# Second attention: a chunk's softmax weights behind the next chunk's rotated rows, their transposes behind its scores

## The reference, cut to what matters

```python
Q = (x @ Wq).reshape(B, T, h, k).transpose(0, 2, 1, 3)
K = (x @ Wk).reshape(B, T, g, k).transpose(0, 2, 1, 3)
V = (x @ Wv).reshape(B, T, g, k).transpose(0, 2, 1, 3)
...
Q = Q * cos + rotate_half(Q) * sin
K = K * cos + rotate_half(K) * sin
scores = jnp.einsum('bhqk,bhsk->bhqs', Q, K) / jnp.sqrt(jnp.float32(k))
scores = jnp.where(causal[None, None], scores, -jnp.inf)
A = jax.nn.softmax(scores, axis=-1)
Y = jnp.einsum('bhqs,bhsk->bhqk', A, V)
...
h = h + _L1_attn_ref(_layernorm(h, axis=-1), ...)
```

## Time and profile before

| | |
|---|---|
| runs before, us | 1389.83 median of 3 (1388.47 to 1391.47) |
| the profiled execution, us | 1393.95, its span 1391.8 |
| TensorE matmuls busy | 1228.5 us, 88% of the span |
| VectorE, ScalarE, GpSimd busy | 864.6, 613.2, 231.8 us |
| TensorE busy from 1040 to 1190 us (the second attention) | 115.45 of 150 us, mean granted clock 0.78 |
| VectorE busy there | 104.86 of 150 us |

### The profile page before, as it was taken

The page is one execution under the profiler, slowest core; times in us unless marked ns, Lnnn a source line. Parts: engine busy times, 40 slices in busy tenths (PEclk is TensorE's granted clock), DMA queues, the critical chain, the costliest instruction groups (busy, mean ns, idle before and its releaser), DMA issues.

```text
span 1391.8 us, 30551 instructions
## 1 busy us (share of the span) xinstructions
PE 1228.5 (88%) x10764; PEld 718.6 (52%) x10778; DVE 864.6 (62%) x1767; ACT 613.2 (44%) x1054; POOL 231.8 (17%) x280
## 2 busy tenths in 40 slices
PE   5999899999999999957799999999957885959997
PEld 2447566666666666635344444444524664424443
DVE  5985454655546555488844454554357677778886
ACT  3444444544445444425244444444423332246664
POOL 2220000000000000000123333333258600110000
PEclk9997999999999999986999999999977887989998
DMA  5121452444524435214147767775247700000000
GB/s 196 61 83 49 154 202 109 181 175 162 198 109 181 181 145 210 107 46 185 46 150 251 265 218 279 262 253 183 92 129 135 105 7 2 1 1 16 23 23 27
DMA packets 43277, 180.98 MB, mean 130 GB/s; under 512 B 9172, under 2 KB 10512, under 8 KB 35408
## 3 DMA queue, kind: packets, MB, share of 16 engines
q0 software_dynamic: 19744, 95.41, 20.7%
q1 hardware_dynamic: 20016, 72.15, 14.6%
q10 hardware_dynamic: 3456, 12.58, 2.5%
HBM read 132.39 MB, written 47.73 MB: 129 GB/s over the span
## 4 chain that ended last, share of the span: by engine, by line
PE 52%; DVE 24%; issue 13%; ACT 4%; POOL 2%; DMA 2%; DVEq 1%; another core or an unknown queue 0%; SPq 0%; ACTq 0%; POOLq 0%
PE ps L935 14%; PE ps L937 13%; PE ps L936 13%; DVE rs L1611 2%; PE ps L1049 2%; DVE ff L2043 2%; DVE amf L2050 2%; PE ps L1028 1%; PE ps L1123 1%; PE ps L1376 1%; DVE we_sp L1405 1%; DVE bst L1478 1%; PE ps L1264 1%; ACT vp L682 1%; PE ps L1358 1%
## 5 line engine op out<-in xcount | busy, mean ns | idle before, releaser
L935 PE MATMUL ps<-nT_hi,wa_hi 128*128 128x368 f16 x576 | 189.2, 328 | 11.8 <-DVE wa_lo L1405 7.7
L936 PE MATMUL ps<-nT_lo,wa_hi 128*128 128x368 f16 x576 | 188.8, 328 | 0.0
L937 PE MATMUL ps<-nT_hi,wa_lo 128*128 128x368 f16 x576 | 188.1, 327 | 0.0
L1772 DVE SCALAR_TENSOR_TENSOR nrm<-ps,xg,nrm 128x256 f32<-128x256 f32 x61 | 29.5, 483 | 122.9 <-ACT nrm L749 103.1
L523 POOL DMA_INDIRECT xg<-xrow,idx x61 | 61.2, 1004 | 263.4 <-PE ps L1123 113.8
L935 PE MATMUL ps<-wide,xT 128*128 x244 | 92.7, 380 | 13.8 <-issue 9.3
L1605 DVE SCALAR_TENSOR_TENSOR a<-sq,eps_row,E 128x184 f32<-128x184 f32 x32 | 13.1, 409 | 131.3 <-ACT sq L699 131.3
L1579 DVE SCALAR_TENSOR_TENSOR wide<-ps,wide 128x368 f32<-128x368 f32 x128 | 66.8, 537 | 42.0 <-PE ps L937 42.0
L936 PE MATMUL ps<-wide,xT 128*128 x244 | 92.5, 379 | 0.0
L937 PE MATMUL ps<-wide,xT 128*128 x244 | 92.5, 379 | 0.0
L1358 PE MATMUL ps<-qw,qT 128*128 128x512 bf16 x372 | 85.6, 383 | 4.0 <-DVE ff L2043 2.6
(11 more groups left out here) (317 smaller groups left out, 2893.6 us busy)
## 6 DMA issues: line engine op xcount, KB each, us to landing
we_st<-in_we POOLq DMA_DIRECT2D x16, 1536.0 KB, 6.8
wsp<-we_sp POOLq DMA_DIRECT2D x16, 1536.0 KB, 5.4
wide<-wsp SPq DMA_DIRECT2D x16, 1536.0 KB
yslot<-yt POOLq DMA_DIRECT2D x61, 256.0 KB
wq_st<-in_ffq SPq DMA_DIRECT2D x24, 512.0 KB, 4.5
wq_st<-in_ffq ACTq DMA_DIRECT2D x24, 512.0 KB, 3.5
wide<-in_wa SPq DMA_DIRECT2D x10, 1024.0 KB, 6.9
xt<-in_x SPq DMA_DIRECT2D x12, 512.0 KB, 3.5
```

The lines of the kernel that those rows point to most:

```text
L935: nc.tensor.matmul(dst, lhs[0], rhs[0], start=start, stop=False)
L936: nc.tensor.matmul(dst, lhs[0], rhs[1], start=False, stop=False)
L937: return nc.tensor.matmul(dst, lhs[1], rhs[0], start=False, stop=stop)
L1772: V.scalar_tensor_tensor(ht, ps[:, 2 + p, FI:2 * FI], AS / WS if x is None else xgw[:, x, ds(D + e, 1)], sgt[:, p, :], ALU.mult, ALU.mult) ...
```

## The change

Only orders change; no instruction is added, removed or resized. In chunks 1 to 3 VectorE's `weights(c - 1)` moves from before rotation 2 to behind `rotated(c)` and the row tiles' `low`, just ahead of `centred(c)`. In chunks 1 and 2 `group_stats` moves ahead of rotation 1, `group_shift` stands behind rotation 1 (and `y_low`), and `low(k)` behind rotation 3. On TensorE `turn(c - 1)` moves behind `scores(c)`, the row turns k+1 and k+2 come directly behind the value projection and lose their wait for ScalarE's evictions of the weights, and the turn waits for `low` of tile k+2 in place of k. ScalarE empties the row turns before the weights' turns. Chunk 0 and the turn of the last chunk stay as they are.

```diff
@@ ScalarE
                 moved(c, 5)
-                if c:
-                    weights_turned(c - 1)
                 if inner:
                     high(k + 1)
                     high(k + 2)
...
+                if c:
+                    weights_turned(c - 1)
                 if c + 1 < CH:
                     moved(c + 1, 0)
                     moved(c + 1, 1)
@@ TensorE
-                if c:
-                    turn(c - 1, k if inner else NT - 1)
                 if inner:
-                    for j in (k + 1, k + 2):
-                        pe.wait_ge(f_pe, ready(4 * (c - 1) + 2 + j % 2))
-                        row_turn_l1(j)
+                    row_turn_l1(k + 1)
+                    row_turn_l1(k + 2)
...
                 scores(c)
+                if c:
+                    turn(c - 1, k + 2 if inner else NT - 1)
                 if c + 1 < CH:
@@ VectorE
                 rotate(c, 0)
+                if inner:
+                    group_stats(c + 1)
                 rotate(c, 1)
...
                 if c > 1:
                     y_low(c - 2)
-                if c:
-                    if c + 1 < CH:
-                        group_stats(c + 1)
-                        group_shift(c + 1)
-                    weights(c - 1)
-                for j in range(2, 5):
-                    rotate(c, j)
-                    if j == 2 and 0 < c < CH - 1:
-                        low(k)
+                if inner:
+                    group_shift(c + 1)
+                rotate(c, 2)
+                rotate(c, 3)
+                if inner:
+                    low(k)
+                rotate(c, 4)
                 rotated(c)
...
+                if c:
+                    weights(c - 1)
                 centred(c)
```

More of the change, by code:

```diff
@@ L1947, in _ @@
                 k = GT * (c + 1)
+                inner = 0 < c < CH - 1
                 rotate(c, 0)
+                if inner:
+                    group_stats(c + 1)
                 rotate(c, 1)
@@ L1955, in _ @@
                     y_low(c - 2)
-                if c:
-                    if c + 1 < CH:
-                        group_stats(c + 1)
-                        group_shift(c + 1)
-                    weights(c - 1)
-                for j in range(2, 5):
-                    rotate(c, j)
-                    if j == 2 and 0 < c < CH - 1:
-                        low(k)
+                if inner:
[5 more added lines that the diff above has]
+                rotate(c, 4)
                 rotated(c)
-                if 0 < c < CH - 1:
+                if c == 0:
+                    group_shift(1)
+                    low(k)
+                if inner or c == 0:
                     low(k + 1)
                     low(k + 2)
[L1969 to L1972, removed]
+                if c:
+                    weights(c - 1)
                 centred(c)
```

## The result

The changed kernel took 1382.32 us (median of 5, 1377.17 to 1383.52) and the kernel before 1391.47 us in the same set of runs; the ratio is 0.9942 with a 95% interval of 0.9925 to 0.9959, so 8.1 us faster (5.7 to 10.4). The medians alone lie 9.2 us apart; I go by the ratio. A second set gave 0.9945 (0.9925 to 0.9966). The forecast was 1383.8 us, a gain of 6.0 us.

A forecast was written before the change was run, and what follows sets the result against it. In the second attention TensorE and VectorE wait for each other in a loop, neither full, with the weights in its path. Chunks 1 to 3 gain 1.1 + 2.6 + 2.3 = 6.0 us: 1389.83 - 6.0 = 1383.8; 8-in-10 range 1380.8 to 1388.2.

The forecast's parts named there:

- VectorE, chunk 2: VectorE's new order in chunk 2 releases the scores 15.5 us after the first rotation (20.9 before); chunk gains 2.6 us in all.
- R: Start of VectorE's first rotation in chunk 2, at 1115.18 before, from which the forecast counts.
- Chunk 3: Rotated rows come earlier and the turn fits into the 3.56 us wait ahead of `weighted`: 2.3 us gained (3.2 to -1.0).
- Chunk 1: Wait before row turn k goes; 0.3 us lost by order, 1.1 gained with the clock's 1.4 (range 3.0 to -1.1).
- Statistics earlier: Chunks 1 and 2, VectorE: statistics start about 4 us behind the last addition's issue; listed among edits that cost nothing.
- at nothing: Forecast's list of moved steps given no gain or cost: later `low(k)`, earlier statistics and root, ScalarE's order.
- The turn and the clock: Turn behind the scores costs 3.83 us; its transposes bring back full clock for the next projection, 1.4 us each in chunks 1 and 2.
- Behind chunk 3: From chunk 3's `weighted` to the output rows: nothing changes, the gain arrives whole, 0 us added.
- (a): Rival: transposes do not raise TensorE's clock, projections stay slow; 3.2 us gained, 1386.6 us; chance 0.14.
- (b): Rival: gain does not show, eaten by the `rotated` wait, late weights or issue gaps; at most 2 us, some 1388.5; chance 0.12.
- (c): Rival: slower, TensorE's clock stays low from the scores on; up to 5.5 us lost, 1395.3; chance 0.08.
- It would wait for `h`, up to 2 us once: Chunk 2, VectorE: earlier statistics wait if the last addition into `h` lands later than about 4 us behind its issue.

The follow-up runs named there:

- threefold turn: Changed kernel with each transpose of the turns behind chunks 1 to 3's scores issued three times; stage 115.5 us, run once for its profile.
- TensorE's order alone: Kernel before with TensorE and ScalarE in the new order, VectorE in the old one; 9.9 us slower than before (6.4 to 13.5).
- early split: Changed kernel with last chunk's weights ahead of chunk 2's low parts, output weights' split ahead of chunk 2's first rotation; ratio 0.9901 to the kernel before.
- projection first in chunk 2: Kernel with last weights first and output weights' split early, plus chunk 2's next projection ahead of the turn; ratio 0.9890 to the kernel before, median 1376.62 us.

## Why the prediction was right, and where it was off

The direction and the size hold: 6.0 us forecast, 8.1 (5.7 to 10.4) measured, 8.5 in the stage. That the time itself came within 1.5 us of 1383.8 is in part luck: the kernel before ran at 1391.47 in this set and not at the 1389.83 that I took off from.

*VectorE, chunk 2.* Right to 0.1 us: `rotated` at R + 15.5, the weights at R + 20.6 (forecast 20.7), the next projection at 24.4 (forecast 24.5), the new wait for `qp` 1.86 (forecast 1.7).

*Chunk 3.* Right: 2.1 for 2.3. The scores ran slower than taken (5.44 for 4.7), `rotated` came a little sooner (13.2 us behind the first rotation for 13.5), the turn hid in the wait.

*Chunk 1* was the term mis-sized, 2.3 for 1.1. I left the value projection at its 6 us; it took 2.9. The scores took 3.77 where I had 6.2. Two waits on VectorE (1.01 and 1.34) took back part of both, as the sum for chunk 2 would have told me had I worked out chunk 1 in the same way. So did the clock behind chunk 0, where nothing was changed: it stayed at 1.2 GHz for 5.7 us of the projections (1074.2 to 1079.9) where it had for 2.5 before (1081.7 to 1084.2), and row turn k came 20.6 us behind the mask, where the sum has 19.2.

*Statistics earlier* stood among the edits "at nothing", with the root's 0.99 and the row turns' 1.2 to 1.4 counted elsewhere and partly traded for the wait for `qp`. Alone it gave 5.8 us (3.6 to 8.2). With the weights late it decides between 110.3 and 104.9 us of stage. This is the larger error: by the sum the gain is chiefly the weights', and the runs give the statistics at least as much of it. By themselves the statistics took 4.7 us off the stage and the weights with the turns 3.1 (timed 5.8 and 4.6, with intervals that overlap); on top of the other they took 5.4 and 3.8.

*The turn and the clock.* The turn cost 3.8 us as taken, and transposes do bring the clock back, as the threefold turn shows; but in chunks 1 and 2 it came back only behind the turn, 2.5 and 1.4 us into the first projection (1101.34 to 1103.80, 1129.67 to 1131.07), so projection and eviction took 4.0 and 3.5 us where 4.6 had been: 0.6 and 1.1 gained for the 1.4 taken twice. What was missing there came in at the scores, at 3.77 and 4.01.

*Behind chunk 3* I forecast nothing and 1.5 us came: `weighted` 1.65 for 2.33, the last turn 3.43 for 3.83, and the last `weighted` 1.7 for some 2.2, all by a higher clock (1.00, 0.58 and 1.00 granted, where it was 0.50, 0.50 and 0.55).

*The signs.* Two of those that I had named went the other way. The turn waited 1.34 and 1.10 us for the weights, where over 1 us was to speak against the forecast: the scores ran faster than taken and no longer covered the weights. And the granted clock was 0.62 and 0.72 over the first projections behind the turns of chunks 1 and 2, not 1.00 in most of both.

*The rivals.* (a) fell by the threefold turn as a mechanism, though of the time that the clock was to give back (1.4 twice) only 1.7 us came. (b), nothing shows, fell; its reason, that VectorE's list leaves little slack, is true, as the waits for `qp` and the weights show. (c) did not come about, though TensorE's order alone shows that it exists. "It would wait for `h`, up to 2 us once" was not met in the changed kernel, and met with 3.3 us as soon as the rotation came 4.4 us earlier. I had counted the margin of 4 us from the issue and not from the landing: with the rotation 0.7 and 1.4 us earlier (early split, projection first in chunk 2) the third tile's statistics already waited 0.26 and 1.09 us.

## What to carry to other kernels

When two engines wait for each other in turn, write each one's list as a sum from one fixed event to the next (here R + 15.5, R + 20.7) for every chunk; that sum was right to a tenth in chunk 2, and in chunk 1, where I left it out, two waits of over 1 us went unseen. A step that feeds a third engine (the request for a root) belongs ahead of work that doesn't need the answer, and may be worth as much as the large step that it stands beside. Before idle time is called room, look at what else releases the next step: here the statistics waited 3.3 us for a transfer as soon as the rotation came 4.4 us sooner.

## What the runs showed of the hardware

A dense row of small matmuls can have gaps without any wait in the program. Chunk 1's value projection took 5.9 to 6.0 us in four profiles with additions by DMA beside it, and 2.9 and 2.8 in the two without them. The additions do not suffice for it: in seven other profiles it took 2.9 us beside them, in the changed kernel at the same granted clock (1.00) and DMA share (0.76 for 0.79). What makes the difference is open.

And f32 transposes bring TensorE's clock from 1.2 back to 2.4 GHz: 48 of them took 8.0 us, with the granted clock at 0.50 when they began and 1.00 before they ended.
